# Two steps of the probability-value product at once, in every second step, in an attention layer

## The reference

```
xn  = layer_norm(x)                       # 8 x 512 x 256
q, k, v = xn @ q_w + q_b, xn @ k_w + k_b, xn @ v_w + v_b
att = softmax(q . k over 16 features, + mask)      # per head 512 x 512
y   = att . v                                      # 8 x 512 x 256
h   = layer_norm(y) * (1 + scale) + shift          # scale, shift from cond
out = x + silu(h) @ out_w + out_b
```

## Time and profile before

| | |
|---|---|
| median of 3 runs | 563.6 us (562.95 to 565.53) |
| profiled execution, its own time | 566.29 us |
| its span, first to last instruction | 564.2 us |
| mean granted TensorE clock | 0.991 |
| shown busy: TensorE, VectorE, ScalarE, GpSimd | 96%, 77%, 66%, 34% of the span |

### The profile page before, as it was taken

The page is one execution under the profiler, slowest core; times in us unless marked ns, Lnnn a source line. Parts: engine busy times, 40 slices in busy tenths (PEclk is TensorE's granted clock), DMA queues, the critical chain, the costliest instruction groups (busy, mean ns, idle before and its releaser), DMA issues.

```text
span 564.2 us, 10272 instructions
## 1 busy us (share of the span) xinstructions
PE 542.6 (96%) x2831; PEld 226.1 (40%) x2834; DVE 435.3 (77%) x914; ACT 370.8 (66%) x674; POOL 192.9 (34%) x238
## 2 busy tenths in 40 slices
PE   6899999999999999999999999999999999998986
PEld 3452334334443344434443344434443344422333
DVE  7299777987869868897869878797869878787525
ACT  2305866777757786687756886677756786675851
POOL 6432302346205522336205422336114432314003
PEclk9989999999999999999999999999999999998999
DMA  5650242332225343242235243242334232241021
GB/s 137 191 164 17 82 123 86 102 107 85 70 85 143 87 112 105 74 139 84 73 94 138 81 119 104 60 137 80 84 102 130 85 85 85 66 142 41 1 76 37
DMA packets 43433, 53.74 MB, mean 95 GB/s; under 512 B 11000, under 2 KB 36728, under 8 KB 43408
## 3 DMA queue, kind: packets, MB, share of 16 engines
q1 hardware_dynamic: 41360, 53.17, 33.1%
q10 hardware_dynamic: 2048, 0.27, 0.3%
HBM read 36.35 MB, written 16.80 MB: 94 GB/s over the span
## 4 chain that ended last, share of the span: by engine, by line
PE 73%; issue 7%; DVE 6%; DMA 5%; SPq 3%; POOL 3%; ACT 2%; POOLq 0%; ACTq 0%; DVEq 0%
PE pv_ps L428 18%; PE mx_ps L395 17%; PE st_ps L412 16%; PE job_ps L470 7%; PE job_ps L504 4%; PE job_ps L477 4%; DMA q_rows<-qk_dram 4%; DVE negmax L711 3%; PE job_ps L492 2%; SPq L1088 2%; POOL qk_parts L964 1%; ACT probs L550 1%; SPq L1091 1%; PE job_ps L487 1%; PE pv_ps L352 1%
## 5 line engine op out<-in xcount | busy, mean ns | idle before, releaser
L711 DVE TENSOR_REDUCE negmax<-mx_ps 128x1 f32<-128x512 f32 x512 | 328.9, 680 | 76.2 <-PE mx_ps L395 72.6
L550 ACT ACTIVATE probs<-st_ps 128x512 f32<-128x512 f32 x512 | 278.5, 598 | 99.2 <-PE st_ps L412 98.5
L395 PE MATMUL mx_ps<-k_rows,q_rows 99*128 99x512 bf16 x512 | 197.0, 385 | 7.1 <-DMA q_rows<-qk_dram 6.3
L412 PE MATMUL st_ps<-q_rows,k_rows 101*128 101x512 bf16 x512 | 194.2, 382 | 2.8 <-ACT probs L550 1.2
L428 PE MATMUL pv_ps<-probs,v_rows 128*32 128x512 f32 x1024 | 137.0, 607 | 0.5 <-ACT probs L550 0.5
L395 PEld LDWEIGHTS mx_ps<-k_rows,q_rows 99*128 99x128 bf16 x512 | 50.6, 99 | 126.6 <-DVE negmax L711 82.6
L955 POOL TENSOR_TENSOR qk_rest<-qk_full,qk_parts 128x512 f32<-128x512 f32 x32 | 37.1, 1159 | 163.4 <-ACT qk_parts L560 163.4
L412 PEld LDWEIGHTS st_ps<-q_rows,k_rows 101*128 101x128 bf16 x512 | 49.9, 98 | 62.6 <-ACT probs L550 23.4
L964 POOL TENSOR_TENSOR qk_parts<-qk_rest,qk_parts 128x512 bf16<-128x512 f32 x32 | 37.1, 1160 | 69.6 <-DVE qk_parts L788 68.6
L470 PE MATMUL job_ps<-x_norm_t,w_qk 128*128 128x512 f32 x128 | 60.7, 596 | 0.0
L571 ACT ACTIVATE qk_full<-job_ps,qkb_col 128x512 f32<-128x512 f32 x32 | 22.0, 687 | 37.9 <-PE job_ps L470 37.9
(11 more groups left out here) (94 smaller groups left out, 392.5 us busy)
## 6 DMA issues: line engine op xcount, KB each, us to landing
qk_dram<-qk_parts SPq DMA_DIRECT2D x96, 128.0 KB
k_rows<-qk_dram SPq DMA_DIRECT2D x32, 192.0 KB
q_rows<-qk_dram SPq DMA_DIRECT2D x32, 192.0 KB
x_in<-in_x SPq DMA_DIRECT2D x16, 256.0 KB, 3.5
k_rows<-qk_dram SPq DMA_DIRECT2D x32, 128.0 KB
q_rows<-qk_dram SPq DMA_DIRECT2D x32, 128.0 KB
x_res<-in_x SPq DMA_DIRECT2D x8, 512.0 KB, 4.5
out<-out_sb SPq DMA_DIRECT2D x16, 256.0 KB, 2.2
```

What stands on the lines that cost most here:

```text
L395: pe.matmul(mx_ps[bank_of(u, MX_BANKS)][:, :], q_rows[0:ROWS_MASK, g, h, c * P:(c + 1) * P], k_rows[0:ROWS_MASK, g, h, :], start=True, sto ...
L412: pe.matmul(st_ps[bank_of(u, ST_BANKS)][:, :], k_rows[0:ROWS_ALL, g, h, c * P:(c + 1) * P], q_rows[0:ROWS_ALL, g, h, :], start=True, stop= ...
L550: act.activation(probs[:, t % P_SLOTS, h, :], st_ps[bank_of(u, ST_BANKS)][:, :], ACT.Exp).then_inc(exp_done, 1)
L711: dve.tensor_reduce(negmax[:, g % 2, h * CH + c:h * CH + c + 1], mx_ps[bank_of(GH * step + h, MX_BANKS)][:, :], AXIS_X, ALU.max, negate=Tr ...
```

## The change

`pv_step` is no longer called in every step with the step before. In every even step it is called twice, for t - 2 and t - 1, and in odd steps not at all. The place within the step stays: between heads 1 and 2, ahead of the MID jobs. The helper now takes the step that it works on, and turns a negative one into a step of the batch before.

```diff
             def pv_step(b, t):
 
-                b, t = (b, t - 1) if t else (b - 1, STEPS - 1)
+                b, t = (b, t) if t >= 0 else (b - 1, t + STEPS)
                 if not exists(b):
                     return
                 g, c = t // CH, t % CH
...
                 for t in range(STEPS):
                     for h in range(GH):
                         if h == GH // 2:
-                            pv_step(b, t)
+                            if t % 2 == 0:
+                                pv_step(b, t - 2)
+                                pv_step(b, t - 1)
                             for n, at_b in jobs_at(b, t, MID):
                                 job(n, at_b)
                         max_unit(b, t, h)
```

## The result

| | before | after |
|---|---|---|
| median of 4 runs each | 563.6 us | 589.1 us (587.88 to 589.34) |
| ratio, 95% interval | 1 | 1.0442 (1.0413 to 1.0472) |
| profiled execution, its own time; span | 566.29; 564.2 us | 588.93; 586.9 us |
| mean granted TensorE clock | 0.991 | 0.991 |

The kernel is 4.4% slower; 587 was forecast. The first look at the profile after is its page: parts 1 and 5 (line, engine, operation, count | busy us, mean ns | idle before, releaser). Lines behind the change stand two further down (L550 is now L552); those of `max_unit`, `st_unit` and `pv_step` keep their numbers.

What follows compares the result with a forecast made beforehand. TensorE sets the pace of a batch, with the row path and buffers tight behind it. Shorts +3.6 and longs -0.8 make +2.8 us a batch, 19.7 for seven, plus 4 in the last: 23.5, so 587 us, range 573 to 598.

Steps and rivals of the forecast that it cites:

- TensorE's own work: Two pv steps together take 1.99 us instead of 2.18: 0.19 saved per pair, 8 pairs a batch, 12 us in all.
- seam: Rival 3: the second pv step of a pair pays 0.19 us of entry and exit itself; 596 us, chance 0.14.
- rival 2: Only TensorE's work counts: path and banks hide, all longs shrink by 1.28 us; 552 us, chance 0.06.
- Shorts: First product of steps 2, 6, 10, 14 to that step's cturn: 1.97 us, each +0.90 with a pair.
- The long from 14: From cturn of step 14 to step 2's first product: 14.23 us now, about 14.2 after, waiting 0.6; gain 0.
- the rows: Split rows of the next head group, 9.2 us from VectorE's cast through writes and reads to TensorE's first product.
- holds: Score products waiting for a PSUM bank that ScalarE's exponential must leave, expected in nearly every odd step, 0.5 to 0.9 in some.
- The long from 2: From cturn of step 2 to step 6's first product: 12.51 to 12.6 us, by a rows floor and bank waits.
- The longs from 6 and 10: From cturn of steps 6 and 10 to the first product four steps on: 14.38 to 14.24, 15.14 to 14.45 us.
- The sum: A batch goes from 64.0 to 66.8 us, +2.8; seven batches 19.7, the last 4, all 23.5 us.
- The clock: Rival 4: TensorE's granted clock falls in the new gaps, 1.7 us once a batch; 600 us, chance 0.07.
- Buffers don't suffice: Denies rival 1, that buffers suffice and longs from 6 and 10 keep the full 1.28 us; 572 us, chance 0.14.

Runs made afterwards that it cites:

- early cast: VectorE's cast of part 1 moved ahead of the reads at head 0: on the changed kernel 582.8 us (1.0325), on the kernel before 560.8 us (0.9920).
- half exponentials: Changed kernel with the exponential of only 256 of 512 score columns, which pv reads twice: 576.1 us, ratio 1.0213.
- early fill: SP issues the row fills of part 0 ahead of the writes of parts 1 and 2: changed kernel 587.3 us (1.0380), kernel before 568.5 us (1.0070).
- late DMAs: Changed kernel with ScalarE's two DMAs behind a cturn issued after the second exponential of the next step: 592.0 us, ratio 1.0509.
- all four edits: Exponentials and maxima over 256 of 512 columns, VectorE's cast and SP's part 0 fills earlier: kernel before 560.5 us (0.9961), changed kernel 558.8 us (0.9915).

## Why the prediction was right

- *TensorE's own work.* The pair takes 1.86 from its first matmul to the next instruction, 1.95 with the 0.09 of entry, against 1.99 forecast and 2.18 apart: 0.23 saved, not 0.19. There is no seam. That half of the drains go is what the Trainium skill, "TensorEngine Tiling (Array Packing)", section Key Properties, leads one to expect, and the trace agrees. The kernel didn't become faster by it: that was rival 2.
- *Shorts.* +0.85 each, forecast +0.90; nothing hid it.
- *The long from 14.* 14.19, no gain, held by the rows: right, and shown by the early cast, which gives 0.66. The 0.6 to 0.8 of waiting that was forecast is 0.72 by starts (the last four matmuls ahead start 2.44 before 380.78, where 1.72 is usual), and 0.35 of it was there before. Ahead of it lie the holds, with the forecast sizes: 0.25 each in steps 15 and 1 for ScalarE's banks, 0.41 for a maximum of VectorE.
- *The long from 2.* 12.61 for 12.6, but for one of two reasons that I gave it. The rows as a floor would have been undone by the early cast, and it stayed at 12.62. It is the holds that fill it, and counted by starts they have the forecast sizes: 0.88 and 0.05 in step 3 for 0.88 and 0.06, and 0.52 and 0.05 in step 5 for 0.51 and 0.06. Of the 0.88, 0.15 is a maximum product waiting for VectorE (319.31), which the working didn't have.
- *The longs from 6 and 10.* The place of the holds was right, steps 8 and 9 the largest and 11 and 13 small. By starts they are 0.52 and 0.63 for 0.57 each, and 0.30 and 0.24 for 0.25 each. The parts came out 0.1 shorter than forecast (14.10 for 14.24, 14.36 for 14.45), since the pair saves 0.04 more, 0.11 was lost in the part from 6 before already (behind the v projection), and the 0.1 behind the v read of step 10 didn't come. The half exponentials show that holds behind ScalarE are the cause. The Trainium skill, "Perfetto Trace Analysis", section Identifying Performance Opportunities, says that a repeated gap on the engine that should be full can mean too few buffers; the trace agrees, with 15.9 us before L412 for 1.2. A third bank for scores wasn't tried.
- *The sum.* 2.5 to 2.6 a batch for 2.8; six full batches 15.7. Two sizes were off in opposite directions, 3.3 too much for seven batches and 2.3 too little for the last, and nearly cancel; that much of the hit is luck. The first batch was counted like the rest, and gave +0.7 up to the first product of step 2 in batch 1. From the first product of step 14 in batch -1 on, the four shorts add 3.4 there, but the longs give back 2.1 and not 1.0; the waiting for rows at that product falls only from 1.26 to 0.92. The other 0.65 was there already (38.20 for 38.85), and is scatter: in the profiled kernels without the early fill this instant lies anywhere from 37.1 to 39.2. The last batch was counted 4 and took 6.3. The clock was left out of the sum, and some 1.7 of the 2.3 is the second fall, in this execution.
- *Rivals.* Buffers don't suffice, there is no seam, and the clock doesn't fall in the gaps of 0.2 to 0.7 within a batch (1.00 in all five windows, and every short with a pair up to the last batch's fall is 2.81 to 2.83). It falls in the last batch, as before.

So where pairing takes 1.32 out of each long, 5.3 a batch, 1.0 was kept. Counted by the distances between TensorE's starts, before and after, the other 4.3 went to holds behind ScalarE (3.4), to waits for VectorE's maxima (0.6) and to longer waiting for the rows (0.3). These stand one behind the other, so taking one away doesn't give back all of it: shorter exponentials bring back 1.6, and in the part from 14 what they free is waited for the rows.

## What to carry to other kernels

A block on the engine that sets the pace also gives the others time to empty their buffers: before merging two blocks to save their entry costs, list what each of them covers, and what ends in the stretches that get shorter. The cost was 3.4 us a batch where a double block stood and 1.0 of 5.3 kept elsewhere, to save 0.23 eight times. A stretch that already ends at a transfer gives nothing back however much work is taken out of it; pull the transfer first (here one cast moved by a few instructions gave 0.8% on the kernel before). And price a hold by the distance of two starts: the idle time in brackets showed 0.56 of a hold of 0.88.

## What the runs showed of the hardware

- A product that waits for a 4 KB transfer issued by ScalarE came 1.79 us behind the issue where SP's two 128 KB writes went out after it, and 2.74 us behind it where they went out 0.15 us before it.
- No length of wait decides in these runs whether the granted clock falls. In the last batch, before the first product of step 6, it fell behind waits of 1.10 and 1.18 us (changed kernel with the early fill, with the late DMAs), 1.60 and 1.69, and not behind 0.91, nor behind 1.85 and 2.16 (kernel before with the early fill, with all four edits). In the changed kernel's last batch it also fell around 554, where the longest wait since 538 is 0.78; in the full batches, waits of 0.2 to 0.7 left it at 1.00.
- The clock differs between executions of one kernel: the changed kernel with the early cast had spans from 576.8 us (mean clock 1.00) to 582.7 (0.985). Differences of 1 us between medians are best read from the parts of a batch at clock 1.00.
